# Where the modulation columns and gate rows are made in a two-layer adaptive-norm transformer kernel

## The reference

```
mod = (silu(c) @ wmod).reshape(4, 6, 1, 256)        # per layer
sa, ca, ga, sb, cb, gb = mod[:, 0..5]
ga, gb = (2*(g >= 0) - 1) * max(|g|, 0.25)          # gates kept away from zero
h = layernorm(x) * (1 + ca) + sa
x = x + ga * attention(h)
h = layernorm(x) * (1 + cb) + sb
x = x + gb * ffn(h)
```

## Time and profile before

| | us |
|---|---|
| median of 3 runs | 1310.63 (1310.13 to 1314.87) |
| the profiled execution | 1310.77 |
| its span in the profile | 1309.0 |
| mean granted TensorE clock | 0.971 of full |

### The profile page before, as it was taken

How to read it: one execution, slowest core, us unless ns; L and a number is a source line. 1 busy time by engine, 2 the same in 40 slices (tenths; PEclk the granted TensorE clock), 3 DMA queues, 4 the chain that set the end, 5 groups by cost and what they waited for, 6 DMA issues and landing times.

```text
span 1309.0 us, 22523 instructions
## 1 busy us (share of the span) xinstructions
PE 1192.1 (91%) x6940; PEld 870.5 (67%) x6940; DVE 935.0 (71%) x2757; ACT 686.7 (52%) x1599; POOL 681.0 (52%) x679
## 2 busy tenths in 40 slices
PE   6888897988569999999999999999999999999998
PEld 5445464545447677686786777867767777667787
DVE  5767787775567786877867868778778687676553
ACT  3356646564354645546546455465465564654432
POOL 0340101011135799998579999857999999000000
PEclk9789999999779999999999999999999999999999
DMA  6431012000124210320420302132022000000000
GB/s 219 132 80 50 26 50 89 26 34 1 65 85 125 76 38 0 135 70 30 139 95 5 129 7 70 49 121 92 26 111 69 2 33 32 0 2 1 17 17 33
DMA packets 36102, 77.93 MB, mean 60 GB/s; under 512 B 8152, under 2 KB 22336, under 8 KB 35248
## 3 DMA queue, kind: packets, MB, share of 16 engines
q1 hardware_dynamic: 26736, 47.13, 10.8%
q0 software_dynamic: 8128, 25.49, 6.0%
q10 hardware_dynamic: 1152, 4.19, 0.8%
HBM read 54.62 MB, written 22.04 MB: 59 GB/s over the span
## 4 chain that ended last, share of the span: by engine, by line
PE 37%; DVE 25%; issue 8%; ACT 3%; DVEq 0%; ACTq 0%
PE bank L1494 10%; PE bank L1468 7%; DVE qk L1093 6%; DVE qkst L1069 5%; PE bank L1479 5%; PE bank L297 5%; PE bank L299 5%; PE bank L298 5%; DVE negmax L1164 2%; DVE probs L1159 2%; DVE x L1149 2%; DVE ytmps L1146 1%; DVE sm L131 1%; DVE sm L129 1%; PE bank L1455 1%
## 5 line engine op out<-in xcount | busy, mean ns | idle before, releaser
L711 POOL TENSOR_SCALAR gtmp<-gidx,lut 128x344 f32<-128x344 int32 (+2 forms) x210 | 299.5, 1426 | 21.3
L1468 PE MATMUL bank<-kT,qT 128*128 128x128 f32 (+3 forms) x512 | 181.7, 444 | 13.2 <-ACT probs L887 13.1
L714 POOL TENSOR_TENSOR gacc<-gacc,gtmp 128x344 f32<-128x344 f32 (+2 forms) x210 | 183.6, 874 | 17.5
L887 ACT ACTIVATE probs<-bank,negmax 128x128 f32<-128x128 f32 (+3 forms) x256 | 135.1, 528 | 60.6 <-DVE negmax L1164 57.0
L297 PE MATMUL bank<-wgH,hL 128*128 128x512 f32 x384 | 155.3, 404 | 1.1 <-issue 1.1
L1164 DVE TENSOR_REDUCE negmax<-bank 128x1 f32<-128x128 f32 (+3 forms) x256 | 122.6, 483 | 42.4 <-PE bank L1469 40.5
L298 PE MATMUL bank<-wgL,hH 128*128 128x512 f32 x384 | 152.3, 397 | 0.0
L299 PE MATMUL bank<-wgH,hH 128*128 128x512 f32 x384 | 152.1, 396 | 0.0
L1494 PE MATMUL bank<-pT,v 128*128 128x512 f32 (+3 forms) x512 | 149.2, 434 | 0.8 <-ACT pT L879 0.7
L1103 DVE TENSOR_REDUCE negmax<-bank 128x1 f32<-128x512 f32 (+3 forms) x176 | 108.1, 636 | 57.4 <-PE bank L1398 57.0
L1069 DVE BATCH_NORM_STATS2 qkst<-qk 128x6 f32<-128x128 f32 x512 | 109.4, 280 | 46.4 <-issue 46.4
(11 more groups left out here) (221 smaller groups left out, 2682.4 us busy)
## 6 DMA issues: line engine op xcount, KB each, us to landing
hH<-h_saved SPq DMA_DIRECT2D x16, 512.0 KB, 4.0
hL<-h_saved SPq DMA_DIRECT2D x16, 512.0 KB, 4.9
qst<-q_parts SPq DMA_DIRECT2D x96, 64.0 KB, 2.4
w_saved<-shi POOLq DMA_DIRECT2D x24, 256.0 KB, 2.3
w_saved<-slo POOLq DMA_DIRECT2D x24, 256.0 KB, 2.6
sraw<-in_wqkv POOLq DMA_DIRECT2D x18, 256.0 KB, 3.0
wgH<-w_saved SPq DMA_DIRECT2D x3, 1536.0 KB, 8.4
wgL<-w_saved SPq DMA_DIRECT2D x3, 1536.0 KB, 11.6
```

The costliest lines, as they stand in the source:

```text
L711: link(pool.tensor_scalar(tmp if j else acc, part, float(j), lut1[0:rows, j:j + 1], ALU.is_equal, ALU.mult))
L714: link(pool.tensor_tensor(acc, acc, tmp, ALU.add))
L1468: pe.matmul(bank[SCORE_BANKS[i % 3]][:, 0:n], qT[:, h, t * P:n], kT[:, h, 0:n], start=True, stop=False)
```

## The change

The three blocks of PE work leave the place ahead of step 0 and become nine pieces in steps 2 to 10, behind the scores of the step: six of four column products (one norm, scale or shift), two pieces of gate rows (two of four rows each), and one for the two rows of L1291. The columns use bank 2, not 4. ACT copies the columns out in step 13, and DVE forms the gates in step 13. PE's wait for the copied columns moves from unit 2 of the scores to the first transposed scores in step 16. Ahead of step 0 DVE makes the norm of batch 1 alone (4 tiles); batches 2 and 3 follow in eight pieces in steps 21 to 28. PE turns batch 1 in step 1, behind the second score unit, not ahead of the first; DVE's low part follows two `n` later. ACT's scaling for the later batches moves from n = 20, 21 to n = 32, 33.

```
+MODS, MODS_READ, NORM_23 = 2, 13, 22
...
-        cols = bank[4][:, 0:2 * 4 * KT * NB].rearrange("p (c i k b) -> p c i k b", c=2, i=4, k=KT)
+        cols = bank[2][:, 0:2 * 4 * KT * NB].rearrange("p (c i k b) -> p c i k b", c=2, i=4, k=KT)
...
-                elif n in (20, 21) and 0 < b < NB - 1:
-                    if n == 20:
+                elif n in (32, 33) and 0 < b < NB - 1:
+                    if n == 32:
                         norm_a0.wait_turned(act, b)
-                    norm_a0.act_scale(act, b + 1, 2, (b + 1) * QT, range(2 * n - 40, 2 * n - 38))
+                    norm_a0.act_scale(act, b + 1, 3, (b + 1) * QT, range(2 * n - 64, 2 * n - 62))
...
-            act.wait_ge(cols_pe, 2)
-            copy_cols(1, 4)
-            act.wait_ge(cols_ready, 4)
...
+                if s == MODS_READ:
+                    act.wait_ge(cols_pe, 2)
+                    copy_cols(1, 4)
...
-                if n == 3:
+                if n == (5 if b == 1 else 3):
                     dve.wait_ge(qkv_pe, b * (KT + 2))
                     norm_a0.dve_low(dve, b, hH2, hL2)
...
+                elif b == 1 and 0 <= n - NORM_23 < NORM_PARTS:
+                    norm_a0.dve_part(n - NORM_23, dve, chains[0], 2, 2 * QT, 2 * QT)
...
-            norm_a0.dve(dve, ch, 1, (NB - 1) * QT, QT)
-            dve.wait_ge(rows_pe, 2)
+            norm_a0.dve(dve, ch, 1, QT, QT)
+            def make_gates():
+                dve.wait_ge(rows_pe, 2)
...
+                if s == MODS_READ:
+                    make_gates()
...
+            def modulations(n):
+                if n == 0:
+                    pe.wait_ge(loaded_m, 32)
+                if n < 6:
+                    last = columns(1 + n // 2, n % 2)
+                    if n == 5:
+                        last.then_inc(cols_pe, 1)
+                elif n < 8:
+                    gate_rows(2 * n - 12)
+                    last = gate_rows(2 * n - 11)
+                    if n == 7:
+                        last.then_inc(rows_pe, 1)
+                else:
+                    for k in range(KT):
+                        last = pe.matmul(bank[3][VW:2 * VW, :], sc[:, 0, k, :], wmod[:, 0, k, SB * D:(CB + 1) * D],
+                                         start=(k == 0), stop=(k == KT - 1))
+                    last.then_inc(rows_pe, 1)
...
-                if n == 0:
+                if n == (2 if b == 1 else 0):
...
                     if b == i == 0:
                         pe.wait_ge(rows_ready, 3)
+                        pe.wait_ge(cols_ready, 4)
...
-                    if b == 0 and i == 2:
-                        pe.wait_ge(cols_ready, 4)
...
+                if 0 <= s - MODS < 9:
+                    modulations(s - MODS)
```

More of the change, by code:

```diff
@@ L796, in after0 @@
                         act.wait_ge(rows_pe, 2)
+                        act.wait_ge(cols_ready, 4)
                     norm_f0.act_mod(act, b)
@@ L968, in _ @@
             dve.wait_ge(loaded_x, 16)
-            norm_a0.dve(dve, ch, 1, (NB - 1) * QT, QT)
-            dve.wait_ge(rows_pe, 2)
[L971 to L981, removed]
+            norm_a0.dve(dve, ch, 1, QT, QT)
+            ch_mod = chains[0]
+            def make_gates():
+                dve.wait_ge(rows_pe, 2)
+                raw = bank[5][:, 0:D]
+                ch_mod.step(dve.tensor_scalar(gsign[:, :], raw, 0.0, 2.0, ALU.is_ge, ALU.mult))
+                ch_mod.step(dve.tensor_scalar(gsign[:, :], gsign[:, :], -1.0, None, ALU.add))
+                ch_mod.step(dve.tensor_tensor(gmag[:, :], raw, gsign[:, :], ALU.mult))
+                dve.scalar_tensor_tensor(out=grows[:, :], in0=gmag[:, :], scalar=0.25, in1=gsign[:, :], op0=ALU.max,
+                                         op1=ALU.mult).then_inc(rows_ready, 1)
+                dve.wait_ge(rows_ready, 1)
+                gb = grows[VW:2 * VW, :]
+                dve.scalar_tensor_tensor(out=gffn[VW:2 * VW, 0:D], in0=bank[3][VW:2 * VW, D:2 * D], scalar=1.0, in1=gb,
+                                         op0=ALU.add, op1=ALU.mult).then_inc(rows_ready, 1)
+                dve.tensor_tensor(gffn[VW:2 * VW, D:2 * D], bank[3][VW:2 * VW, 0:D], gb, ALU.mult).then_inc(rows_ready, 1)
             def after0(n, b):
@@ L1229, in _, with columns, gate_rows @@
         def _(pe):
[L1230 to L1240, removed]
+            def columns(i, kind):
+                l, *cs = NORM_MODS[i]
+                c = cs[kind]
+                for m in range(KT):
+                    for k in range(KT):
+                        last = pe.matmul(cols[:, kind, i, m, :], wmod[:, l, k, c * D + m * P:c * D + (m + 1) * P],
+                                         sc[:, l, k, 0:NB], start=(k == 0), stop=(k == KT - 1))
+                return last
+            def gate_rows(j):
+                l, c = ((0, GA), (0, GB), (1, GA), (1, GB))[j]
+                for k in range(KT):
+                    last = pe.matmul(bank[5][j * VW:(j + 1) * VW, 0:D], sc[:, l, k, :], wmod[:, l, k, c * D:(c + 1) * D],
+                                     start=(k == 0), stop=(k == KT - 1))
+                return last
+            def modulations(n):
[11 more added lines that the diff above has]
+                else:
+                    for k in range(KT):
+                        last = pe.matmul(bank[3][VW:2 * VW, :], sc[:, 0, k, :], wmod[:, 0, k, SB * D:(CB + 1) * D],
+                                         start=(k == 0), stop=(k == KT - 1))
+                    last.then_inc(rows_pe, 1)
             pe.wait_ge(consts, 8)
@@ L1244, in _ @@
             pe.wait_ge(loaded_m0, 16)
-            columns(0, 1)
+            columns(0, 0)
+            columns(0, 1).then_inc(cols_pe, 1)
             def pre0(n, b):
-                if n == 0:
+                if n == (2 if b == 1 else 0):
                     if b:
@@ L1282, in _ @@
                 pre0(n, 0)
[L1283 to L1293, removed]
             def after0(n, b):
```

## The result

The changed kernel is slower. Four runs gave a median of 1327.99 us (1321.85 to 1329.86) against 1310.91 before; the ratio is 1.0116, with a 95% interval of 1.0077 to 1.0154. On two further chips it came to 1.0125 (1.0096 to 1.0154) and 1.0127 (1.0098 to 1.0157). So it is 15 to 17 us above before, where the forecast was 8.0 and the range ended at 1326.

A forecast was written before the change was run, and what follows sets the result against it. Layer 0 was taken as a lockstep with PE busy in 91% of the span, so shifts at step 16 reach the end. Terms -3.6 + 10.1 + 1.0 + 0.5 = +8.0 us on 1310.77 gave 1318.8, range 1309 to 1326.

The forecast's parts named there:

- Term 1: Ahead of step 0 to score unit 2: scores start earlier, with 3.6 us of the lead left at unit 2.
- Term 2: Steps 2 to 10: nine pieces cost 12.8 us at a mixed clock, less 2.7 of waits, +10.1 us.
- low-clock rival: Clock low throughout: term 2 is 14.4 us, up to 5 more for later products; 1323 to 1331, chance 0.17.
- rule of the Trainium skill: Steps 2 to 10: sustained matmul activity lifts the idle engine's low clock, making term 2 8.5 - 2.7 us.
- Term 3: DVE's gates in step 13 delay step 16 by 0.5 us and unit 14's maximum by 0.9; +1.0 taken.
- Term 4: Steps 21 to 28: norms of batches 2 and 3 delay unit 22's maximum, +0.5 us, bounds -0.7 and 3.
- At nothing: POOL's gate traffic, which starts about 25 us later but is first needed in step 73.: POOL's later gate traffic, from step 13's gates to step 73, was counted as costing 0 us.
- "faster" rival: Steps 1 to 10: pieces hidden and batch 1 ready in time, whole 7 us lead kept; 1304, chance 0.05.
- A shift at step 16 reaches the end whole.: Layer 0 is a lockstep of semaphore waits, so any shift at step 16 reaches the end undiminished.

The follow-up runs named there:

- a_mods_ahead: Changed kernel with the nine pieces ahead of step 0 again, the rest as changed: 1316.94 us against 1313.39 for the kernel before, 1.0040.
- the held loads: Changed kernel, POOL's six gate broadcast loads waiting until the second group's maxima have landed: 1322.44 us against 1313.39 before; repeated, 1324.26 against 1313.52.
- the later norms: Changed kernel with gate loads held and the norm pieces of batches 2 and 3 one step later: 1325.04 us against 1312.58 before, 1.0093.
- b_rows_first: Kernel before with gate and modulation rows ahead of the columns, before step 0: 1312.19 us against 1312.58, 0.9990.
- a_filler: Changed kernel with 22 unused products of 512 columns in PE's idle time ahead of step 0: 1325.22 us against 1313.39 before, 1.0092.
- b_loads_held: Kernel before, POOL starting the gates' way through memory only once the first group's maxima have landed: 1319.94 us against 1313.39, 1.0042.
- b_shift: Kernel before with the block of columns ahead of step 0 made twice, shifting everything behind it: 1327.06 us against 1314.03, 1.0111.
- best1: Changed kernel with rows, three column pieces and DVE's gates before step 0, three column pieces in steps 11 to 13: 1310.89 us against 1312.58 before, 0.9983.

## Why the prediction was wrong

- **Term 1, the earlier start, -3.6 us.** Right: -4.2 in the mean. Unit 0 came at 33.0 to 34.0 us; the wait for batch 1 and the low clock of its turn took half of the lead, as worked out.
- **Term 2, nine pieces, +10.1 us.** The mechanism was right, and a_mods_ahead shows it: without the pieces in steps 2 to 10 only 3.6 to 5.3 us of the loss are left. The size depends on the clock. Measured is +12.1 in the mean, in two forms: 24.3 to 24.7 us from unit 2 to unit 11 in two profiles, +10.1, and 28.5 to 28.7 in two, +14.2. In the long form all six column pieces and one gate piece ran at the low level, the low-clock rival's case up to the second q projection. I gave that rival a chance of 0.17, and its time, 1323 to 1331, holds the median; its own terms (14.4, up to 5 more, and the other three) add up to no more than 1328.1. Which form comes seems to be chance: the six long q products of step 5 were followed by the high clock in two profiles (0.89 and 1.00 from 50 to 52 us) and by the low one in the other two. Both profiles of the held loads and the one of the later norms, with the same order on PE up to step 16, took the long form too (28.4 to 28.9 us), so two long ones in four may be too few, and the mean of +12.1 too low by about 1 us. By the rule of the Trainium skill (TensorE: Matmul & The Clock Gate, "What's actually happening"), as the prediction read it, the full steps would have run at the high level. The four profiles speak against that (a granted clock of 0.64 to 0.76 at a PE without a gap), and in b_rows_first the clock fell at 34.8 us without any idle time. The filler doesn't separate idle time from thin work, as its clock fell in a wait.
- **Term 3, gates in step 13, +1.0 us.** Nothing at step 16: it follows unit 11 by 5.9 us, as before, and the last gate instruction ends at 72.05 where the wait ends at 72.15. Unit 14's maximum behind it was late, which shows as 0.8 us two transposed units on. The cast of the keys fell to 0.43 us, as assumed.
- **Term 4, norms, +0.5 us.** Right: a piece of 1.40 us fills an idle time of 0.86, and moving it away takes 0.5 to 0.6 us off the distance between the groups, in one profile.
- **"At nothing: POOL's gate traffic, which starts about 25 us later but is first needed in step 73."** This step failed. I had looked at who needs the data and not at what the loads run beside. Five loads of 256 to 512 KB now fall on the second group's transfers, which stand in PE's way. The profile showed the price of a good place: 2.18 us of waiting for the maxima in the first group. In the changed kernel the four transfers lose 2.4 us in the mean (0.6 to 4.0), and with the loads held they lose nothing. In b_loads_held, where they meet more of the loads, they lose 6.1, and the time rises by 6.5 us (3.1 to 7.9). A start that moves by 25 us had to be laid over the next transfer that somebody waits for.
- **Two slips beside the sum.** On the page the clock's first dip lies in slices 2 and 3, not 2 to 4, and the "faster" rival's 1304 leaves out terms 3 and 4. Neither moves the forecast.
- **"A shift at step 16 reaches the end whole."** Right for a delay, as a lower bound: b_shift's 10.5 us arrive, with 2 to 3 on top. Not borne out for a lead: best1's 4.2 us at the first group and 5.7 at the second gave 1.7 in time (0.3 to 4.2).

Of the 13.1 us in the profiles, 11.5 are there when the second group starts (-4.2 + 12.1 - 0.1 + 3.6, rounded); the other 1.6 lie within the spread of single profiles. Against the forecast of 8.0 the profiles have 5.1 us more: 2.0 from the clock in term 2, 2.6 at the second group, nearly all of it the gate traffic, and 1.6 behind it, less 0.6 each for the earlier start and for step 16. The 2 to 4 us by which the medians exceed the profiles stay open. They go with the granted clock: the changed kernel's timed runs have a median clock of 0.962 and before's 0.968 or 0.969, but its columns alone lengthen the low stretches, and the long form may be the more frequent one. Why a pure shift costs more than itself was not settled.

## What to carry to other kernels

Moving work off a path that is exposed into steps that look slack pays only for the slack that is there: here 2.7 us of named waits stood against an estimated 12.8 us of work, and the work went ahead of the one unit on which the next transfer hung. Put such pieces behind the instruction that starts the transfer, where the engine idles anyway: best1 does that, and its gain of 1.7 us is barely clear of none. When a block moves, follow the transfers that it triggers to where they land: a load that nobody needs for 60 us can still stop the engine if it runs beside a 2 KB transfer that somebody waits for.

## What was not expected of the hardware

- Four transfers of 2 KB, which take 3.75 us from the first issue to the products that need them, took 7.78 and 9.89 us when five broadcast loads of 256 to 512 KB ran beside them, and 4.36 us in another profile of the same changed kernel.
- The granted clock went from 1.00 to 0.50 and stayed there for 12 us in a_filler, though PE was busy in 11.72 of them; and in b_rows_first it fell while products of 512 columns ran (3.50 us for four records that take 1.88 in best1) and rose as 4-column products began.
- One and the same stretch of the same kernel took 24.35 and 28.73 us in two profiles, with the granted clock at 0.76 and 0.64, and single runs of the changed kernel lie between 1319.97 and 1335.41 us. A single profile of a kernel whose clock toggles is a sample.
